# The last product of both down stages in two passes: two tiles first, then one tile after another

## The chip, the cores and the metric

One core of a Trainium2 chip runs the whole kernel. The metric is device time in microseconds (us) of one execution, median of several runs. Lower is better.

## The reference

A decoder layer on x of 2 x 512 tokens by 1024 features, in three parts: a state-space mixer with a gated feed-forward, a quantized product with a context matrix, and a second gated feed-forward whose weights are built from two arrays each. Both feed-forwards have 3584 inner features. In outline:

```python
x = x + mamba_and_gated_mlp(layernorm(x))   # silu(h2 @ gate_w.T) * (h2 @ up_w.T) @ down_w.T
x = x + quantized_product(layernorm(x), ctx_4096)   # fake_quant both, then matmul
# _L0_ffn_ref(layernorm(x), ...)
W1, W2, W3 = (base + mean(abs(w - base)) * sign(w - base) for each pair)
h = silu(hidden @ W1.T) * (hidden @ W3.T)   # 1024 tokens, 1024 -> 3584
x = x + h @ W2.T                            # 3584 -> 1024
```

All of it is fp32 within a small tolerance.

## The kernel before

Feature tiles of 128 lie on the partitions and tokens on the free axis. fp32 products are made of three rounded matmuls each (fp32r): high weight by high activation, high weight by low activation, low weight by high activation. ScalarE makes the high part of each operand by a copy, VectorE the low part by a subtraction.

The kernel runs in stages: head and mixer, feed-forward m=0, the context product, feed-forward m=1. A feed-forward has a gate-and-up part and a down part. The down stage uses a seven-product scheme on 2 x 2 blocks (Strassen's kind, with sums of blocks formed on VectorE), for two halves of the inner features (`sc` = 0 and 1), so it has 14 products, `d` = 0 to 13. One product has `SC_PAIRS` = 7 steps `k`, one for each pair of inner tiles, and `KH` = 4 output tiles `q` of 128 x 512, each in a bank of PSUM of its own: banks 0 to 3 for even `d`, 4 to 7 for odd `d`. In `down_step` (L1071) one step is 4 tiles of 3 matmuls, so a product is 7 x 12 = 84 matmuls.

Work orders:

- A step needs a slot of the weight ring (`ring_hi`, `ring_lo`; `RING` = 7) and one of the inner ring (`inner_ring_a`, `inner_ring_b`; 7 too). VectorE's `feed_forward` (L1949) and ScalarE's (L1458) fill the slots five or six steps ahead of TensorE, in an order written out by hand. A slot is refilled when its step of the product before is done (`s_pd`, one count per step; L1322, L1350, L1796).
- `down_out` (L1901) waits on VectorE for the end of a product and adds or subtracts its four tiles into x (`x_mid` for m=0, `x_last` for m=1), one instruction of 128 x 512 per tile (L1915), each with one count of `s_do`. TensorE needs these counts before it writes the banks again, two products later.
- At the end of m=1, SyncE stores each tile of the last quarter when its count of `s_do` is there (L736 to L740), and then the program ends.
- At the end of m=0, TensorE's order (L1155 to L1170) weaves the start of the context stage into the last product: the matmuls for a mean (L1157) stand before step 3, and the sums for a variance (`ctx_var`, L1119) before step 5. The mean waits for `s_xs`, which VectorE counts at the end of `x_sum_of` (L1965, L1994), done after `down_out` of product 12. The variance waits for four sums of squares, `square_pairs` (L2287) on VectorE, which come after `ctx_centre` (L2269), and that waits for the mean. After the last product TensorE does 64 small matmuls for column sums (L1111), the second mean (L1170, L1173, which wait for `s_do`), the first context products (L1125), column sums again and a second variance (L1119).
- VectorE leaves its feed-forward loop for m=0 six steps before the end (L1987), when the last slots are filled, and then goes through L2330 to L2337: centring, pairs, constants, root, two rounding steps (L2303), `down_out` of the last product, the other rounding steps. ScalarE's root for the second variance is L1619, behind a pass over the columns (L1635).
- SyncE loads `raw_even` (L685) for the next feed-forward when `s_pd` says that the whole down stage is done; VectorE uses it with the signs in L1947.

TensorE's order at the end of m=0:

```python
        feed_forward(BASE_G[0] + 2, W_END[0] - 4)
        pe.wait_ge(s_xs, 1)
        pe.matmul(bank(0), ones_mean[:, :], scr_c(4)[:, HALF[0]], start=True, stop=True).then_inc(s_hm, 1)
...
        feed_forward(W_END[0] - 4, W_END[0] - 2)
        ctx_var(bank(1), x_square_a, range(KH), KT, (), 0)
        feed_forward(W_END[0] - 2, W_END[0])
```

Of the kernel before, what the change touches and what calls it, by code (L numbers as in the profile page):

```python
# [11 lines left out]
P = 128  # L12
# [175 lines left out]
def build(nc, x_t, ctx, w_mamba, w_dt, w_gu, w_dn, f_gu, f_dn, b_gu, b_dn, params, shapes_only,  # L188
# [233 lines left out]
    s_dtm, s_dte, s_dts, s_csx = (sem(n) for n in ("dt_and_cs_summed", "dt_exp_in", "dt_and_cs_act", "cs_exp_in"))  # L422
    s_dtc = sem("dt_rows_copied")
    s_hpair = sem("head_pairs_summed")
# [33 lines left out]
    s_ld = [[sem(f"down_in{g}_{k}") for k in range(SC_PAIRS)] for g in range(2)]  # L458
    s_xq = [sem(f"x_quarter_in{i}") for i in range(4)]
    s_do, s_x2, s_out = sem("down_taken"), sem("x2_stored"), sem("out_stored")  # L460

# [364 lines left out]
    def _(pe):  # L826
# [72 lines left out]
        conv_pair(1)  # L899
        pe.wait_ge(s_dtc, 1)  # L900
        pe.wait_ge(s_ht, BATCH + 1)
# [113 lines left out]
        def product(w, m, p, t, x):  # L1015
# [53 lines left out]
            ins.then_inc(s_pd, 1)  # L1069

        def down_step(w, m, sc, t, k):  # L1071

            pe.wait_ge(s_wlo, w + 1)
            u = w - BASE_D[m]
            pe.wait_ge(s_ulo, m * ND + u + 1)
            d = sc * 7 + t
            if k == 0:
                if d >= 2:
                    pe.wait_ge(s_do, 4 * (m * 14 + d - 1))
                elif d == 0:  # L1080
                    pe.wait_ge(s_c12, 2 * (PAIRS - 1) * (m + 1))
                else:
                    pe.wait_ge(s_gs, 4 * PAIRS * (m + 1))
                    pe.wait_ge(s_pr[2], PAIRS * (m + 1))
                    if m == 0:
                        pe.wait_ge(s_ab, CF_BLOCKS)
            slot, us = w % RING, u % RING
            for q in range(KH):
                out = bank(4 * (d % 2) + q)
                col = slice(q * P, (q + 1) * P)  # L1090
                for n, (wt, a) in enumerate(((WRH, ur_hi(us)), (WRH, ur_lo(us)), (WRL, ur_hi(us)))):
                    ins = pe.matmul(out, wt[:, slot, col], a, start=t in (0, 1, 3) and k == 0 and n == 0,  # L1092
                                    stop=k == SC_PAIRS - 1 and n == 2, skip_group_check=True)
            ins.then_inc(s_pd, 1)
# [143 lines left out]
    def _(act):  # L1238
# [277 lines left out]
        act.wait_ge(s_dtm, 1)  # L1516
        act.activation(dt_rows, ps[2][0:2 * HEADS, :], ACT.Copy).then_inc(s_dtc, 1)
        root(1, scr_u)
# [164 lines left out]
    def _(dve):  # L1683
# [217 lines left out]
        def down_out(w):  # L1901
# [5 lines left out]
            for quad, op in {0: ((0, ALU.add),), 1: ((0, ALU.add),), 2: ((1, ALU.add),), 3: ((3, ALU.subtract),),  # L1907
                             4: ((3, ALU.subtract),), 5: ((1, ALU.add),), 6: ((2, ALU.subtract),)}[t]:
                dve.wait_ge(s_xq[quad], 16 * (m + 1))
                if d % 14:  # L1910
                    dve.wait_ge(s_do, 4 * d)
                dve.wait_ge(s_pd, w + 1)
                for q in range(KH):
                    tile = X[m][:, QROW[quad] + q, COL[m][QCOL[quad]]]
                    TT(tile, tile, bank(4 * ((sc * 7 + t) % 2) + q), op).then_inc(s_do, 1)  # L1915
# [206 lines left out]
        TS(ncs_all[:, :, :], ncs_all[:, :, :], -1.0, None, ALU.mult).then_inc(s_dte, 1)  # L2122
        dve.wait_ge(s_dts, 1)

# [7 lines left out]
        own.then(TT(ncs_all[:, :, :], ncs_all[:, :, :], dend_all[:, :, :], ALU.mult))  # L2132
        dve.wait_ge(s_dts, 3)
        own.then(TT(ncs_all[:, :, :], ncs_all[:, :, :], gtot_all[:, :, :], ALU.mult))
# [21 lines left out]
        conv_pair(CONV_TILES // 2 - 1, decay_rows)  # L2156
        dve.wait_ge(s_dts, 5)
        dve.wait_ge(s_silu, CONV_TILES)
# [279 lines left out]
```

## Time and profile before

| what | value |
|---|---|
| median of 3 runs | 2155.32 us (2153.18 to 2155.93) |
| the profiled execution | 2155.74 us, span of its instructions 2153.9 us |
| mean granted TensorE clock | 0.991 of 2.4 GHz |
| TensorE busy | 2105.2 us, 98% of the span |
| VectorE busy | 1664.3 us, 77% |
| ScalarE busy | 1070.0 us, 50% |
| DMA | 370.06 MB, mean 172 GB/s |

The times inside the profile are us from the start of the span. The first down stage ends at about 1260, the second at about 2149. A timeline row has its start, its length, the engine, the source line and operation, what was written and read, and how many instructions it merges; in brackets stands how long the engine sat idle before it, and who released it. The lengths of TensorE's matmuls overlap, so their pitch is read from the starts. "Granted clock" (PEclk) is the share of 2.4 GHz that TensorE was given: 1.00 is 2.4 GHz, 0.50 is 1.2 GHz.

### The profile page before, as it was taken

The page shows a single profiled execution, that of the slowest core. Times are in us where ns is not written, and L with a number is a line of the kernel's source. Part 1 is how long each engine was busy: PE and PEld are TensorE (multiplying, and loading weights), DVE is VectorE, ACT ScalarE, POOL GpSimd, SP SyncE. Part 2 cuts the span into 40 slices and gives each one's busy share as a digit, 9 for nine tenths or more (in the row PEclk, how much of TensorE's full clock was granted, in tenths as well). Part 3 has the DMA queues.
Part 4 walks back from the last instruction along what each step waited for, and adds up shares of the span by engine and source line. Part 5 has one row for each costly group of instructions (what it writes and reads, how often), then busy time and mean ns, then how long its engine had stood idle before and what let it go on. Part 6 is the DMA issues. An engine that isn't in the chain of part 4 may idle for free.

```text
span 2153.9 us, 26614 instructions
## 1 busy us (share of the span) xinstructions
PE 2105.2 (98%) x9266; PEld 1684.2 (78%) x9270; DVE 1664.3 (77%) x2497; ACT 1070.0 (50%) x1764; POOL 182.1 (8%) x296
## 2 busy tenths in 40 slices
PE   7999999999999999999999999899999999999999
PEld 3777778778888878888888854788888888888887
DVE  7776666698777878887979898887777677788885
ACT  4333344457777777774444466443333333444442
POOL 0000110101111111210000002001000000100000
PEclk9999999999999999999999999999999999999999
DMA  3151115638989999888250044554444444756101
GB/s 123 40 186 50 57 59 175 171 75 287 311 294 309 344 320 328 307 308 337 90 184 1 1 166 105 152 186 152 159 171 147 164 147 147 287 194 197 63 20 59
DMA packets 136434, 370.06 MB, mean 172 GB/s; under 512 B 16688, under 2 KB 27568, under 8 KB 132656
## 3 DMA queue, kind: packets, MB, share of 16 engines
q1 hardware_dynamic: 111216, 288.16, 39.1%
q0 software_dynamic: 25088, 80.23, 11.0%
q8 instruction: 73, 1.20, 0.2%
q14 instruction: 57, 0.47, 0.1%
HBM read 288.12 MB, written 84.41 MB: 173 GB/s over the span
## 4 chain that ended last, share of the span: by engine, by line
PE 82%; DVE 10%; ACT 4%; issue 2%; DMA 2%; SPq 0%; DVEq 0%; ACTq 0%
PE pair L1067 41%; PE pair L1092 24%; PE pair L839 6%; PE pair L832 2%; PE pair L1011 2%; DVE conv_out L2099 1%; DMA ctx_in<-ctx 1%; DVE ring_lo L1779 1%; PE pair L949 1%; DVE pair L1923 1%; PE pair L970 1%; PE pair L848 1%; DVE weights_lo L1689 1%; PE pair L1125 1%; PE pair L972 0%
## 5 line engine op out<-in xcount | busy, mean ns | idle before, releaser
L1067 PE MATMUL pair<-comb_hi,ring_hi 128*128 128x512 f32 x1456 | 567.3, 390 | 3.3 <-ACT gate_a L1401 3.3
L1067 PE MATMUL pair<-comb_hi,ring_lo 128*128 128x512 f32 x1456 | 567.2, 390 | 0.0
L1067 PE MATMUL pair<-comb_lo,ring_hi 128*128 128x512 f32 x1456 | 567.1, 389 | 0.0
L1092 PE MATMUL pair<-inner_ring_a,ring_hi 128*128 128x512 f32 x1120 | 344.8, 389 | 0.0
L1067 PEld LDWEIGHTS pair<-comb_hi,ring_hi 128*128 128x128 f32 x1456 | 273.7, 188 | 61.7 <-DVE ring_lo L1779 4.9
L1067 PEld LDWEIGHTS pair<-comb_hi,ring_lo 128*128 128x128 f32 x1456 | 273.7, 188 | 57.0
L1067 PEld LDWEIGHTS pair<-comb_lo,ring_hi 128*128 128x128 f32 x1456 | 273.7, 188 | 56.6
L1092 PEld LDWEIGHTS pair<-inner_ring_a,ring_hi 128*128 128x128 f32 x1120 | 210.2, 188 | 43.5
L1092 PE MATMUL pair<-inner_ring_a,ring_lo 128*128 128x512 f32 x560 | 217.9, 389 | 0.0
L1323 ACT ACTIVATE ring_hi<-ring_sum 128x512 fp32r<-128x512 f32 x160 | 101.0, 632 | 142.0 <-DVE ring_sum L1764 140.3
L1092 PE MATMUL pair<-inner_ring_b,ring_hi 128*128 128x512 f32 x448 | 138.3, 390 | 0.0
L1779 DVE TENSOR_TENSOR ring_lo<-raw_a,ring_hi 128x512 fp32r<-128x512 f32 x146 | 99.4, 685 | 50.1 <-ACT ring_hi L1323 50.1
L1449 ACT ACTIVATE sign_out<-pair 128x1024 int8<-128x1024 f32 x84 | 85.9, 1023 | 80.7 <-DVE pair L1923 80.7
L1092 PEld LDWEIGHTS pair<-inner_ring_a,ring_lo 128*128 128x128 f32 x560 | 105.1, 188 | 21.9
L839 PE MATMUL pair<-act_hi,weights_hi 128*128 128x512 f32 x256 | 109.3, 427 | 1.6 <-DVE act_lo L2168 1.4
L1779 DVE TENSOR_TENSOR ring_lo<-ring_sum,ring_hi 128x512 fp32r<-128x512 f32 x160 | 109.5, 684 | 1.5 <-ACT ring_hi L1323 0.2
L1923 DVE TENSOR_TENSOR pair<-coeff_in 128x1024 f32<-128x1024 f32 x84 | 103.0, 1226 | 0.8 <-DMA coeff_in<-b_gu 0.8
L1689 DVE TENSOR_TENSOR weights_lo<-weights_raw,weights_hi 128x1024 fp32r<-128x1024 f32 x44 | 54.6, 1240 | 59.5 <-ACT weights_hi L1246 31.1
L839 PE MATMUL pair<-act_hi,weights_lo 128*128 128x512 f32 x256 | 100.3, 392 | 0.0
L839 PE MATMUL pair<-act_lo,weights_hi 128*128 128x512 f32 x256 | 100.1, 391 | 0.0
L1092 PEld LDWEIGHTS pair<-inner_ring_b,ring_hi 128*128 128x128 f32 x448 | 84.1, 188 | 17.8 <-issue 0.5
L1323 ACT ACTIVATE ring_hi<-raw_a 128x512 fp32r<-128x512 f32 x146 | 90.3, 625 | 8.4 <-PE pair L1011 5.6
(374 smaller groups left out, 3586.1 us busy)
## 6 DMA issues: line engine op xcount, KB each, us to landing
coeff_in<-f_gu SPq DMA_DIRECT2D x56, 512.0 KB, 5.2
coeff_in<-b_gu SPq DMA_DIRECT2D x56, 512.0 KB, 6.8
weights_raw<-w_mamba SPq DMA_DIRECT2D x44, 512.0 KB, 3.4
raw_a<-w_gu SPq DMA_DIRECT2D x28, 512.0 KB, 7.3
raw_a<-w_gu SPq DMA_DIRECT2D x56, 256.0 KB, 6.3
u_spill<-gate_a POOLq DMA_DIRECT2D x56, 256.0 KB, 5.8
coeff_in<-f_dn SPq DMA_DIRECT2D x28, 512.0 KB, 4.4
coeff_in<-b_dn SPq DMA_DIRECT2D x28, 512.0 KB, 6.6
```

The costliest lines, as they stand in the source:

```text
L832: ins = pe.matmul(out[:, HALF[half]], w[:, wi, k * P:(k + 1) * P], a(half, k), start=k == 0 and n == 0, stop=k == KT - 1 and n == 2)
L839: ins = pe.matmul(out, w[:, wi, k * P:(k + 1) * P], a(b, k), start=k == 0 and n == 0, stop=k == KT - 1 and n == 2, skip_group_check=True)
L848: return pe.matmul(out[:, HALF[b]], ones[:, :], src[:, HALF[b]], start=first, stop=last)
L949: pe.matmul(ps[2][:, g * 512:(g + 1) * 512], bx_cur[:, 2 + g, :], xbc[:, 4 + g * HPG:4 + (g + 1) * HPG, b * SEQ + c * P:b * SEQ + (c + 1) ...
L1011: ins = pe.matmul(out, wt[:, slot, col], a, start=j % 2 == 0 and kk == 0 and n == 0, stop=j % 2 == 1 and kk == KH - 1 and n == 2, skip_gro ...
L1067: ins = pe.matmul(out, wt[:, slot, col], a, start=t in (0, 1, 3) and kk == 0 and n == 0, stop=kk == KH - 1 and n == 2, skip_group_check=True)
L1092: ins = pe.matmul(out, wt[:, slot, col], a, start=t in (0, 1, 3) and k == 0 and n == 0, stop=k == SC_PAIRS - 1 and n == 2, skip_group_chec ...
L1323: act.activation(WRH[:, slot, :], src, ACT.Copy).then_inc(s_whi, 1)
L1449: act.activation(sign_out[:, c % 2, :], dif_ps[:, :], ACT.Sign).then_inc(s_sign, 1)
L1689: TT(WL[:, slot, :], raw[:, rslot, :], WH[:, slot, :].bitcast(F32), ALU.subtract).then_inc(s_ready, 1)
L1779: TT(WRL[:, slot, :], src, WRH[:, slot, :].bitcast(F32), ALU.subtract).then_inc(s_wlo, 1)
L1923: TT(dif_ps[:, :], dif[:, c % 2, 0, :], dif[:, c % 2, 1, :], ALU.subtract).then_inc(s_cd, 1)
```

## The change

The last product of each down stage (`d` % 14 = 13) is done in two passes. While its seven slots come in, only tiles 0 and 1 are multiplied, 6 matmuls a step. Behind the last step tile 2 is done over all seven slots and then tile 3, 21 matmuls each. A new semaphore `s_last` counts when tiles 0 and 1 are done and when tile 2 is done; VectorE waits for it ahead of tiles 0 and 2, and for `s_pd` ahead of tile 3. The seven counts of `s_pd` for this product now come during tile 3. The orders of TensorE, VectorE and ScalarE around it are as they were. `s_dtc` is removed: its one count in the mixer goes to `s_dts`, whose later thresholds rise by one.

```diff
--- before.py
+++ after.py
@@ -420,7 +420,6 @@
     s_hs, s_hfree = sem("hs_ready"), sem("h_region_free")
     s_conv, s_silu = sem("conv_summed"), sem("conv_silu")
     s_dtm, s_dte, s_dts, s_csx = (sem(n) for n in ("dt_and_cs_summed", "dt_exp_in", "dt_and_cs_act", "cs_exp_in"))
-    s_dtc = sem("dt_rows_copied")
     s_hpair = sem("head_pairs_summed")
     s_stage, s_bx, s_rr = sem("chunk_stage_free"), sem("bx_chunk_ready"), sem("cs_rhs_ready")
     s_yt, s_cs, s_ecs, s_msk, s_dec = sem("y_taken"), sem("cs_rows"), sem("exp_cs"), sem("cs_masked"), sem("decay_ready")
@@ -457,6 +456,7 @@
     s_uo = [sem(f"inner_stored{i}") for i in range(4)]
     s_ld = [[sem(f"down_in{g}_{k}") for k in range(SC_PAIRS)] for g in range(2)]
     s_xq = [sem(f"x_quarter_in{i}") for i in range(4)]
+    s_last = sem("last_tiles_done")
     s_do, s_x2, s_out = sem("down_taken"), sem("x2_stored"), sem("out_stored")
 
     block = nc.Block()
@@ -897,7 +897,7 @@
                                 start=False, stop=k == KT - 1, skip_group_check=True)
         ins.then_inc(s_dtm, 1)
         conv_pair(1)
-        pe.wait_ge(s_dtc, 1)
+        pe.wait_ge(s_dts, 1)
         pe.wait_ge(s_ht, BATCH + 1)
         for t in range(NC):
             ins = pe.matmul(ps[3][:, t * 2 * HEADS:(t + 1) * 2 * HEADS], dt_rows[:, t * P:(t + 1) * P],
@@ -1068,6 +1068,21 @@
                                     stop=kk == KH - 1 and n == 2, skip_group_check=True)
             ins.then_inc(s_pd, 1)
 
+        def last_tiles(w, m, k, qs):
+            slot, us = w % RING, (w - BASE_D[m]) % RING
+            for q in qs:
+                out = bank(4 + q)
+                col = slice(q * P, (q + 1) * P)
+                for n, (wt, a) in enumerate(((WRH, ur_hi(us)), (WRH, ur_lo(us)), (WRL, ur_hi(us)))):
+                    ins = pe.matmul(out, wt[:, slot, col], a, start=False,
+                                    stop=k == SC_PAIRS - 1 and n == 2, skip_group_check=True)
+                if k == SC_PAIRS - 1 and q == 1:
+                    ins.then_inc(s_last, 1)
+                elif k == SC_PAIRS - 1 and q == 2:
+                    ins.then_inc(s_last, 1)
+            if qs == (3,):
+                ins.then_inc(s_pd, 1)
+
         def down_step(w, m, sc, t, k):
 
             pe.wait_ge(s_wlo, w + 1)
@@ -1084,6 +1099,14 @@
                     pe.wait_ge(s_pr[2], PAIRS * (m + 1))
                     if m == 0:
                         pe.wait_ge(s_ab, CF_BLOCKS)
+            if d % 14 == 13:
+
+                last_tiles(w, m, k, (0, 1))
+                if k == SC_PAIRS - 1:
+                    for q in (2, 3):
+                        for kk in range(SC_PAIRS):
+                            last_tiles(w - k + kk, m, kk, (q,))
+                return
             slot, us = w % RING, u % RING
             for q in range(KH):
                 out = bank(4 * (d % 2) + q)
@@ -1514,7 +1537,7 @@
 
         conv_silu(0, 0)
         act.wait_ge(s_dtm, 1)
-        act.activation(dt_rows, ps[2][0:2 * HEADS, :], ACT.Copy).then_inc(s_dtc, 1)
+        act.activation(dt_rows, ps[2][0:2 * HEADS, :], ACT.Copy).then_inc(s_dts, 1)
         root(1, scr_u)
         conv_silu(0, 1)
 
@@ -1909,8 +1932,15 @@
                 dve.wait_ge(s_xq[quad], 16 * (m + 1))
                 if d % 14:
                     dve.wait_ge(s_do, 4 * d)
-                dve.wait_ge(s_pd, w + 1)
+                if d % 14 < 13:
+                    dve.wait_ge(s_pd, w + 1)
                 for q in range(KH):
+                    if d % 14 == 13 and q == 0:
+                        dve.wait_ge(s_last, 2 * m + 1)
+                    elif d % 14 == 13 and q == 2:
+                        dve.wait_ge(s_last, 2 * m + 2)
+                    elif d % 14 == 13 and q == 3:
+                        dve.wait_ge(s_pd, w + 1)
                     tile = X[m][:, QROW[quad] + q, COL[m][QCOL[quad]]]
                     TT(tile, tile, bank(4 * ((sc * 7 + t) % 2) + q), op).then_inc(s_do, 1)
 
@@ -2120,7 +2150,7 @@
         own.then(TT(dtf, dtp[:, :, 1, :], dtf, ALU.add))
         own.then(STT(ncs_all[:, :, :], dtf, -1.0, dtf, ALU.mult, ALU.max))
         TS(ncs_all[:, :, :], ncs_all[:, :, :], -1.0, None, ALU.mult).then_inc(s_dte, 1)
-        dve.wait_ge(s_dts, 1)
+        dve.wait_ge(s_dts, 2)
 
         TS(a_all[:, :, :], ncs_all[:, :, :], 1.0, None, ALU.add).then_inc(s_dte, 1)
         dve.wait_ge(s_dte, 2)
@@ -2130,7 +2160,7 @@
         own.then(TS(dend_all[:, :, :], dend_all[:, :, :], 2.0 ** -30, None, ALU.max))
         own.then(dve.reciprocal(dend_all[:, :, :], dend_all[:, :, :]))
         own.then(TT(ncs_all[:, :, :], ncs_all[:, :, :], dend_all[:, :, :], ALU.mult))
-        dve.wait_ge(s_dts, 3)
+        dve.wait_ge(s_dts, 4)
         own.then(TT(ncs_all[:, :, :], ncs_all[:, :, :], gtot_all[:, :, :], ALU.mult))
         own.then(TT(ncs_all[:, :, :], ncs_all[:, :, :], sp1v, ALU.add))
         own.then(STT(dtf, dtf, 0.0, ncs_all[:, :, :], ALU.max, ALU.add))
@@ -2154,7 +2184,7 @@
             ins = dve.tensor_copy(cs_wide[:, :, first:first + HEADS], ncs_all[:, :, :])
         ins.then_inc(s_csx, 1)
         conv_pair(CONV_TILES // 2 - 1, decay_rows)
-        dve.wait_ge(s_dts, 5)
+        dve.wait_ge(s_dts, 6)
         dve.wait_ge(s_silu, CONV_TILES)
         def make_y(h, k):
             y = xbc[:, 4 + k, HALF[ORDER[h]]]
```

## Rows read from the trace of the kernel before

**Rows 1.** The page: busy time by engine, and the chain that ended last, by engine.

```profile
PE 2105.2 (98%) x9266; PEld 1684.2 (78%) x9270; DVE 1664.3 (77%) x2497; ACT 1070.0 (50%) x1764; POOL 182.1 (8%) x296
...
PE 82%; DVE 10%; ACT 4%; issue 2%; DMA 2%; SPq 0%; DVEq 0%; ACTq 0%
```

**Rows 2.** Timeline, TensorE, end of the first down stage: start us, length us, what.

```profile
1235.61 0.62 PE L1092 MATMUL pair<-inner_ring_a,ring_hi 128*128 128x512 f32 x2
...
1236.29 0.62 PE L1092 MATMUL pair<-inner_ring_a,ring_hi 128*128 128x512 f32 x2
...
1243.78 1.02 PE L1157 MATMUL pair<-scratch_c,ones_over_dm 128*128 128x512 f32 x2
...
1250.59 3.59 PE L1119 MATMUL pair<-x_mid,ones_over_dm 128*128 128x512 f32 x8
...
1259.51 1.75 PE L1111 MATMUL pair<-ones_bf,q 128*128 128x1 bf16 x64
...
1261.92 1.10 PE L1170 MATMUL pair<-scratch_c,ones_over_dm 128*128 128x512 f32 x2 [0.66 <-DVE x_mid L1915]
...
1276.49 1.75 PE L1111 MATMUL pair<-ones_bf,q 128*128 128x1 bf16 x64
...
1278.10 3.68 PE L1119 MATMUL pair<-x_mid,ones_over_dm 128*128 128x512 f32 x8
```

**Rows 3.** Timeline, VectorE, the same stretch.

```profile
1238.42 2.87 DVE L1994 TENSOR_TENSOR scratch_c<-scratch_c,x_mid 128x512 f32<-128x512 f32 x4
...
1243.62 0.68 DVE L1810 TENSOR_TENSOR inner_ring_b<-inner_ring_b_f,inner_ring_b 128x512 fp32r<-128x512 f32 x1
...
1244.84 4.87 DVE L2269 TENSOR_TENSOR centred<-x_mid,pair 128x512 f32<-128x512 f32 x8 [0.53 <-PE pair L1157]
...
1249.63 2.49 DVE L2287 TENSOR_TENSOR x_mid<-x_mid 128x512 f32<-128x512 f32 x4
...
1261.09 2.47 DVE L1915 TENSOR_TENSOR x_mid<-x_mid,pair 128x512 f32<-128x512 f32 x4
...
1280.23 2.46 DVE L1947 SCALAR_TENSOR_TENSOR raw_even<-sign_in_ab,coeff,raw_even 128x1024 f32<-128x1024 int8 x2
```

**Rows 4.** Timeline, VectorE, end of the program.

```profile
2134.52 0.68 DVE L1810 TENSOR_TENSOR inner_ring_b<-inner_ring_b_f,inner_ring_b 128x512 fp32r<-128x512 f32 x1
...
2148.75 2.48 DVE L1915 TENSOR_TENSOR x_last<-x_last,pair 128x512 f32<-128x512 f32 x4 [13.55 <-PE pair L1092]
```

**Rows 5.** What line 739 stored, and how long its transfers took.

```profile
L739 SPq DMA_DIRECT2D out_t<-x_last x16: 332/332/338, 2054.5 to 2151.3; - x16
...
DMA to landing us min/median/max: 2.0/2.2/2.3
```

**Rows 6.** Timeline, ScalarE, behind the second variance.

```profile
1279.55 2.56 ACT L1635 ACTIVATE centred<-centred,column_terms 128x512 f32<-128x512 f32 x4 [0.93 <-DVE column_terms L2310]
...
1282.02 0.66 ACT L1619 ACTIVATE scratch_c<-pair,quant_columns 128x512 f32<-128x512 f32 x1
```

**Rows 7.** Stretches: length, busy us by engine, PEclk, DMA share, GB/s.

```profile
13.10:15.20 2.10, 0.00 (x0) 0.00 (x0) 2.05 (x4) 0.63 (x2) 0.00 (x0) 1.00 1.06 403
...
15.30:19.00 3.70, 3.70 (x9) 1.76 (x10) 3.70 (x7) 3.70 (x7) 0.00 (x0) 1.00 0.82 322
...
25.80:29.90 4.10, 0.02 (x1) 0.00 (x0) 4.00 (x7) 1.20 (x3) 0.00 (x0) 0.81 0.22 68
...
29.90:35.10 5.20, 5.18 (x6) 2.18 (x7) 5.20 (x8) 4.17 (x7) 0.00 (x0) 0.50 0.12 49
...
1319.70:1321.50 1.80, 0.04 (x1) 0.00 (x0) 1.80 (x4) 1.26 (x2) 0.00 (x0) 1.00 0.29 107
...
1321.90:1325.40 3.50, 3.50 (x5) 1.35 (x4) 3.40 (x7) 1.41 (x3) 0.00 (x0) 0.51 0.14 53
...
1245.00:1259.50 14.50, 14.50 (x58) 10.43 (x57) 12.16 (x23) 6.71 (x11) 0.00 (x0) 1.00 0.84 291
```

**Rows 8.** Timeline, DMA queue, the load behind the first down stage.

```profile
1259.75 0.33 SPq L685 DMA_DIRECT2D raw_even<-b_gu  x1
```

## The prediction

> **What bounds the kernel now.** The page comes first: TensorE is busy 98% of the span and carries 82% of the chain that ended last [rows 1]. So time is won or lost where TensorE stands, or where the chain leaves it. The change touches two such places, and the timelines of TensorE and VectorE are read there: the end of the first down stage, which runs into the context stage, and the end of the second, which is the end of the program. In the first, three matmuls take 0.68 us (1235.61 to 1236.29), 0.227 each, and TensorE has a little work of the next stage woven in: the mean at 1243.78, the variance at 1250.59 [rows 2]. VectorE, not TensorE, holds the chain there: it comes to the four subtractions of the last product only at 1261.09, behind centring and rounding [rows 3], while TensorE had finished that product at 1259.51 [rows 2]. At the end of the program VectorE does wait for TensorE, 13.55 us, and then runs four subtractions from 2148.75 for 2.48 us, with a store after each [rows 4].
>
> **The second down stage: a gain.** The matmuls are the same 84 in another order, so TensorE ends at the same time unless a slot is late. Slots are now wanted every 6 matmuls (1.36 us) instead of every 12 (2.72). Counting back from 2148.7, the product begins 84 x 0.227 = 19.1 us earlier, at 2129.6. The last slot (number 6) is wanted at 2129.6 + 6 x 1.36 = 2137.8; VectorE starts its last piece at 2134.52 and needs 0.68, so it is ready at 2135.2 [rows 4], 2.6 us early; slot 5 was made 1.2 us before that and is wanted 1.36 us earlier, about as early. No stall: 0. After the last matmul one subtraction is left instead of four; they are 0.60 us apart (2.48 for four, the last 0.68), so 1.8 us go. The stores take 2.0 to 2.3 us to land [rows 5]; the last one now goes alone, which is worth 0 to 0.3 more. I take 1.8: the landings hardly differ. The first three stores go out earlier, under matmuls, on a queue that has nothing else then.
>
> **The first down stage: a loss.** The same order meets the woven-in work. TensorE starts the product at 1235.61. Three steps are now 18 matmuls, 4.1 us, so it stands at the mean at 1239.7. The mean needs the sum over x_mid, VectorE L1994, which ends at 1238.42 + 2.87 = 1241.29 [rows 3]. Idle 1: 1.6 us, where before TensorE came at 1243.78. The mean and its two small neighbours take 1243.78 to 1250.59 less 24 matmuls (5.44), 1.37 us; two steps of two tiles are 2.72 more: TensorE is at the variance at 1245.4.
>
> The variance needs the sums of pairs of squares, VectorE L2287. Centring (L2269) started at 1244.84 because it waited for the mean; its mean is now early, but VectorE must still finish the last slot (L1810, from 1243.62, next start 0.60 later), so centring moves only from 1244.84 to about 1244.3 [rows 3]. The first pair was done at 1249.63 + 0.68 = 1250.3 and now is at 1249.8. Idle 2: 1249.8 less 1245.4, 4.4 us. Before, TensorE covered this wait with whole steps; now each step has half as many matmuls in it, and tiles 2 and 3, which would have covered it, stand behind the variance. From here TensorE is continuous: variance 3.48 (1250.59 to 1259.51 less 5.44), two steps 2.72, tile 2 and tile 3 with 21 matmuls each, 4.76 apiece. End of the product: 1265.5 instead of 1259.5.
>
> Who waits: VectorE, at 0.5 us earlier than before, finds tiles 0 to 2 done and waits about 4 us for tile 3, with all its rounding (L2303) queued behind. TensorE itself goes on with 64 column sums (1.75 us) and comes to the second mean, which started at 1261.92 after 0.66 us of idling for VectorE [rows 2], at about 1267.3: 1.6 + 4.4 - 0.66 = 5.4 us later. Does that last? Up to 1278.10 TensorE has the means, the first products and the second column sums back to back (1261.92, 1276.49, 1278.10 [rows 2]), at its own pace, so the next variance is 5.4 us later too, and ScalarE's root (L1619) hangs on it. That root started at 1282.02, 0.2 us after the variance's last matmul (1278.10 + 3.68), but the column pass L1635 ahead of it ended only at 1282.11 [rows 6]: 0.3 us of slack. Everything up to the next feed-forward hangs on that root; I let 5.1 us through.
>
> **The clock.** A new idle stretch has a second price. The granted clock was full before the idle stretches of 4.1 us (at 25.8) and 1.8 us (at 1319.7); it then fell to 0.50 for 5.2 and 3.5 us of the work behind them, that is 1.2 GHz instead of 2.4; behind an idle stretch of 2.1 us (at 13.1) it stayed at 1.00 [rows 7]. Work at half clock loses half of that time: 1.7 to 2.6 us. For 4.4 us of idling I take 2.3, nearer the row of 4.1 us. The bounds are 0 (the row at 13.1) and 3.4 (two low stretches as at 1319.7). TensorE is continuous behind it, so it all arrives: the product ends near 1268. The Trainium skill (TensorE: Matmul & The Clock Gate, Part 1) says that the throttled state is the default and activity lifts it; its section on HAM oscillation warns of just such gaps inside a loop. By that rule alone the work behind Idle 2 would surely run at 1.2 GHz and rival (a) would have no chance; the trace agrees at 25.8 and 1319.7 and not at 13.1, so (a) keeps one. On the pitch of back-to-back matmuls the same page (Wait, 56ns, not 53.3ns?) gives 215.7 ns for 512 columns, where the rows show 227; an estimate by it puts the end of the product 0.6 us earlier, since 54 matmuls stand behind the variance, and the time at 2160.3.
>
> **The rest of the diff.** The product's counter s_pd now rises only during tile 3. Its waiters: no slot is refilled in this product (all seven are distinct, and the refills look at the product before); the next stage's weights come long after; SP's load of raw_even (1259.75 [rows 8]) waits for the whole product in both versions and moves by some 8 us with the sign and down loads behind it. They are 3.7 MB, 12.6 us at the 291 GB/s of the stretch before [rows 7], so down by about 1281, and L1947 uses them at 1280.23 [rows 3], itself some 7 us later: 0, with 0 to 1 as bounds. The two extra counter steps are carried by matmuls: 0. Merging s_dtc into s_dts changes only thresholds, in the same order: 0.
>
> **Sum.** -1.8 + 5.1 + 2.3 = +5.6 us. The profiled execution took 2155.74, so 2161.3; the median of the runs shown is 2155.32, 0.4 lower, so **2160.9 us**. A measurement of this kernel can tell about 0.2% (4.3 us) from no change; 5.6 is just beyond.
>
> **Rivals.**
> (a) The clock doesn't fall, or falls only inside the idle stretch: +3.3, 2158.6. For it: the row at 13.1, half as long. Against: the one stretch as long as this, at 25.8, was followed by a low clock, and so was the shorter one at 1319.7 [rows 7]. Chance 0.13.
> (b) The first stage's loss is hidden: if the chain from 1261 on were VectorE's and ScalarE's alone, with TensorE 5 to 8 us ahead of them, only the gain at the end would be left: -1.8, 2153.5. For it: VectorE holds the chain at 1261.09, and three of four tiles are ready for it. Against: TensorE is back to back from 1261.92 to 1278.10, and tile 3 itself is late for VectorE. It decides if TensorE has more than 8 us of slack before 1282; the rows show 0.3. This is the one that ends on the other side. Chance 0.15.
> (c) The late TensorE work costs more than once: a second low clock in the rounding stage, whose short matmuls leave gaps of their own, 1.7 us more, or late loads for L1947, 1 us: +7.3 to +8.3, up to 2163.6. Chance 0.1.
> (d) Slots 5 and 6 stall the second stage's last product: it decides if VectorE were 2.6 us later than it is, and then costs what is over. Chance 0.02; about 2162.
> The forecast keeps 0.6.
>
> **How the numbers follow.** The forecast's own spread is the clock term, 1.7 to 3.4 about 2.3, and about 1 us between executions: 2159.5 to 2163. With (a) and (d) that is 0.75; to hold 0.8 the range takes in most of (c) and the partly hidden cases towards (b): 2156.5 to 2163.5. Slower by over 4.3 us: nine tenths of the forecast (0.54), (c) and (d), 0.66. Faster by over 0.2% needs more than twice the end's gain with nothing lost, a quarter of (b): 0.04. The rest of (b), (a) and the forecast's tail are 0.30.
>
> **What will show it.** In the changed profile: TensorE idle about 1.6 us before L1157 and about 4.4 us before L1119, releaser VectorE; a granted clock of 0.5 behind the second; the last matmul of the product near 1268 and VectorE's fourth subtraction just behind it, apart from the third; L1619 about 7 us later; the gap kept until the next feed-forward; and at the end of the program a single subtraction after the last matmul. Wrong if TensorE's idling before L1119 is under 2 us, if the root at L1619 moves by less than 3, or if the second stage's last product has a gap.

## The result, and the profile after

The changed kernel takes **2158.94 us** (median of 13 runs, 2157.62 to 2162.62), the kernel before in the same series 2155.32 (13 runs, 2152.74 to 2158.77). The medians are 3.6 us apart; the ratio is 1.0021 with an interval of 1.0013 to 1.0028, which is 2.8 to 6.0 us slower about a middle of 4.5. The interval lies wholly above 1, so the kernel is slower, by about the 0.2% that the prediction called tellable. The forecast was 2160.9.

Two profiled executions can't be subtracted as they stand: everything ahead of the change came 1.40 us earlier in this one. The anchor used from here on is VectorE's four subtractions of the product before the last, 0.3 us behind the start of the last product. In the first down stage they start at 1235.91 before and 1234.51 after. Counted from this anchor A, the changed kernel differs like this:

| from A to | before | after | difference |
|---|---|---|---|
| end of the last product, first stage | 23.60 | 31.36 | +7.76 |
| ScalarE's root | 46.11 | 52.88 | +6.77 |
| the same subtractions of the second down stage | 893.80 | 900.60 | +6.80 |
| from those to VectorE's last subtraction or group of them | 19.04 | 18.94 | -0.10 |
| from the start of that to the end of the span | 5.15 | 3.15 | -2.00 |

With the 1.40 ahead of it: -1.40 + 6.80 - 0.10 - 2.00 = +3.30, the difference of the two spans (2157.2 and 2153.9). Without the 1.40, which the change did not bring, it is +4.7.

The page of the changed kernel, its busy times and its chain, answers to [rows 1]:

```profile
span 2157.2 us, 26618 instructions
...
PE 2108.3 (98%) x9270; PEld 1683.7 (78%) x9270; DVE 1664.7 (77%) x2497; ACT 1070.2 (50%) x1764; POOL 182.1 (8%) x296
...
PE 85%; DVE 9%; ACT 3%; issue 2%; DMA 1%; SPq 0%; DVEq 0%; ACTq 0%
```

Nothing of it tells where the time went; TensorE's share of the chain only rose from 82 to 85%. The timeline does. TensorE of the changed kernel at the end of the first down stage, in place of [rows 2] (line numbers have moved: L1077 is the two-pass product, L1180 the mean, L1142 the variance, L1134 the column sums, L1193 the second mean):

```profile
1234.21 0.62 PE L1077 MATMUL pair<-inner_ring_a,ring_hi 128*128 128x512 f32 x2
...
1239.95 1.12 PE L1180 MATMUL pair<-scratch_c,ones_over_dm 128*128 128x512 f32 x2 [1.50 <-DVE scratch_c L2024]
...
1248.34 5.40 PE L1142 MATMUL pair<-x_mid,ones_over_dm 128*128 128x512 f32 x8 [4.06 <-DVE x_mid L2317]
...
1265.87 1.75 PE L1134 MATMUL pair<-ones_bf,q 128*128 128x1 bf16 x64
...
1267.48 1.10 PE L1193 MATMUL pair<-scratch_c,ones_over_dm 128*128 128x512 f32 x2
...
1283.68 3.68 PE L1142 MATMUL pair<-x_mid,ones_over_dm 128*128 128x512 f32 x8
```

Two brackets are new: 1.50 us ahead of the mean and 4.06 us ahead of the variance, both released by VectorE. And the variance's eight matmuls take 5.40 us where they took 3.59. The bracket of 0.66 before the second mean is gone. VectorE in the same stretch, in place of [rows 3] (L1945 is a subtraction of the product from x, L2024 the sum over x_mid, L2299 centring, L2317 the squares):

```profile
1234.51 2.48 DVE L1945 TENSOR_TENSOR x_mid<-x_mid,pair 128x512 f32<-128x512 f32 x4 [0.85 <-PE pair L1115]
1237.03 2.87 DVE L2024 TENSOR_TENSOR scratch_c<-scratch_c,x_mid 128x512 f32<-128x512 f32 x4
...
1242.82 4.87 DVE L2299 TENSOR_TENSOR centred<-x_mid,pair 128x512 f32<-128x512 f32 x8
1247.60 2.50 DVE L2317 TENSOR_TENSOR x_mid<-x_mid 128x512 f32<-128x512 f32 x4
...
1259.23 1.28 DVE L1945 TENSOR_TENSOR x_mid<-x_mid,pair 128x512 f32<-128x512 f32 x2
...
1261.30 0.69 DVE L1945 TENSOR_TENSOR x_mid<-x_mid,pair 128x512 f32<-128x512 f32 x1 [0.80 <-PE pair L1077]
...
1266.06 0.69 DVE L1945 TENSOR_TENSOR x_mid<-x_mid,pair 128x512 f32<-128x512 f32 x1 [4.07 <-PE pair L1077]
...
1284.85 2.46 DVE L1977 SCALAR_TENSOR_TENSOR raw_even<-sign_in_ab,coeff,raw_even 128x1024 f32<-128x1024 int8 x2
```

VectorE is continuous from the anchor to the squares, so centring comes only 0.62 us sooner after the anchor (8.31 against 8.93) though its mean is there long before: VectorE sets the time of the variance, and TensorE, which now comes early, only waits longer. Tile 3 is the late one (4.07 us). The formation of the next weights (1284.85) waited for no load. The clock, in stretches of TensorE in the changed kernel (columns as in [rows 7]):

```profile
1244.30:1248.30 4.00, 0.00 (x0) 0.00 (x0) 4.00 (x8) 4.00 (x7) 0.00 (x0) 1.00 0.90 315
1248.30:1253.20 4.90, 4.86 (x9) 2.08 (x9) 4.49 (x10) 0.19 (x2) 0.00 (x0) 0.65 1.03 383
1253.20:1265.80 12.60, 12.60 (x56) 10.09 (x54) 5.80 (x9) 3.25 (x5) 0.00 (x0) 1.00 0.22 81
```

In the idle stretch itself the granted clock is still full; in the 4.9 us behind it, it is 0.65 on average, and then full again. Last the end of the program on VectorE of the changed kernel, in place of [rows 4]:

```profile
2135.11 2.48 DVE L1945 TENSOR_TENSOR x_last<-x_last,pair 128x512 f32<-128x512 f32 x4 [0.85 <-PE pair L1115]
...
2139.92 0.69 DVE L1833 TENSOR_TENSOR inner_ring_b<-inner_ring_b_f,inner_ring_b 128x512 fp32r<-128x512 f32 x1
...
2144.64 1.28 DVE L1945 TENSOR_TENSOR x_last<-x_last,pair 128x512 f32<-128x512 f32 x2 [4.03 <-PE pair L1077]
2149.30 0.69 DVE L1945 TENSOR_TENSOR x_last<-x_last,pair 128x512 f32<-128x512 f32 x1 [3.38 <-PE pair L1077]
2154.05 0.69 DVE L1945 TENSOR_TENSOR x_last<-x_last,pair 128x512 f32<-128x512 f32 x1 [4.07 <-PE pair L1077]
```

One subtraction is left behind the last matmul, and the span ends 3.15 us after its start, not 5.15 after that of a group of four. The product did not stall for slots: from A's counterpart in this stage (the four subtractions at 2135.11) to the last subtraction it is as long as before to 0.1 us.

### The profile page after: what moved, and what is told of

The parts are those of the page before. It is cut to its first block, busy times and chain, and to the rows that moved or that the text cites. A ratio compares the mean times of both kernels' runs of the same rounds, so it can differ in the third digit from the quotient of the medians.

```text
span 2157.2 us, 26618 instructions
## 1 busy us (share of the span) xinstructions
PE 2108.3 (98%) x9270; PEld 1683.7 (78%) x9270; DVE 1664.7 (77%) x2497; ACT 1070.2 (50%) x1764; POOL 182.1 (8%) x296
## 4 chain that ended last, share of the span: by engine, by line
PE 85%; DVE 9%; ACT 3%; issue 2%; DMA 1%; SPq 0%; DVEq 0%; ACTq 0%
PE pair L1067 42%; PE pair L1115 23%; PE pair L839 6%; PE pair L1011 2%; PE pair L832 2%; PE pair L1077 1%; DVE conv_out L2129 1%; PE pair L1148 1%; PE pair L1142 1%; PE pair L949 1%; PE pair L848 1%; DVE ring_lo L1802 1%; DVE pair L1953 1%; PE pair L970 1%; DVE weights_lo L1712 1%
## 5 line engine op out<-in xcount | busy, mean ns | idle before, releaser
L1115 PE MATMUL pair<-inner_ring_a,ring_hi 128*128 128x512 f32 x1040 | 320.0, 389 | 0.0
L1115 PEld LDWEIGHTS pair<-inner_ring_a,ring_hi 128*128 128x128 f32 x1040 | 195.2, 188 | 40.6
L1115 PE MATMUL pair<-inner_ring_a,ring_lo 128*128 128x512 f32 x520 | 202.3, 389 | 0.0
L1115 PE MATMUL pair<-inner_ring_b,ring_hi 128*128 128x512 f32 x416 | 128.0, 389 | 0.0
L1115 PEld LDWEIGHTS pair<-inner_ring_a,ring_lo 128*128 128x128 f32 x520 | 97.6, 188 | 20.3
L1346 ACT ACTIVATE ring_hi<-comb_hi_f 128x512 fp32r<-128x512 f32 x72 | 45.4, 630 | 94.4 <-PE pair L1115 48.4
```

The costliest lines, as they stand in the source:

```text
L1346: act.activation(WRH[:, slot, :], src, ACT.Copy).then_inc(s_whi, 1)
```

## The experiments

The theory: the second stage gains 1.8 to 2.0 us, the first loses about 5 by TensorE's idling for VectorE's statistics and about 2 by the low clock behind it, and both arrive at the end. The rival that ends on the other side: the loss of the first stage is hidden behind VectorE and ScalarE. Each median is of a kernel's own runs (number in brackets), its ratio against runs of the kernel before on the same chip (22 to 29 of them, one where there is no interval).

| kernel | median | ratio | interval | in us | root later by |
|---|---|---|---|---|---|
| m1_only | 2152.97 (11) | 0.9988 | 0.9979 to 0.9997 | -2.6 | +0.01 |
| m0_only | 2161.79 (6) | 1.0033 | 1.0021 to 1.0046 | +7.1 | +6.46 |
| count_only | 2154.53 (11) | 0.9998 | 0.9989 to 1.0007 | -0.4 | +1.50 |
| filled | 2157.62 (11) | 1.0012 | 1.0003 to 1.0021 | +2.6 | +5.08 |
| covered | 2153.63 (12) | 0.9996 | 0.9988 to 1.0005 | -0.9 | +0.75 |
| late | 2157.59 (10) | 1.0009 | 1.0000 to 1.0018 | +1.9 | +4.18 |
| mean_earlier | 2151.61 (11) | 0.9990 | 0.9982 to 0.9999 | -2.2 | -0.62 |
| one_first | 2152.27 (1) | | | | +0.01 |
| pair_last | 2153.70 (1) | | | | +1.52 |
| after_again | 2159.31 (11) | 1.0023 | 1.0014 to 1.0032 | +5.0 | +6.76 |
| mean_again | 2152.25 (12) | 0.9982 | 0.9973 to 0.9990 | -3.9 | -0.62 |

"In us" is the ratio's distance from 1 times 2155. "Root later by" is the distance from the anchor A to ScalarE's root in the profiled execution, less the 46.11 of before.

**The change in one stage alone.** `m1_only` keeps the two passes for the second down stage, `m0_only` for the first; the semaphore's thresholds follow.

```diff
-            if d % 14 == 13:
+            if d % 14 == 13 and m == 1:
...
```

> Only the second down stage's last product is done in two passes; the first is as before. Theory (the change is a gain of about 2 us at the end of the program and a loss of about 7 us at the end of the first down stage): 1.8 to 2.1 us faster than the kernel before, so a ratio near 0.999, and from the start of the last subtraction to the end of the span about 3.1 us instead of 5.2. Rival (splitting costs TensorE something of its own, so the loss is in both stages): no faster than the kernel before.

> Only the first down stage's last product is done in two passes. Theory: all of the loss and none of the gain, 5 to 7 us slower than the kernel before, with TensorE idle about 1.5 and 4.1 us in that product and full clock lost behind the second. Rival (the loss comes from elsewhere, or is mostly run to run): within 2 us of the kernel before.

TensorE and VectorE of m0_only, the variance of the first stage and the end of the program:

```profile
1249.87 5.11 PE L1142 MATMUL pair<-x_mid,ones_over_dm 128*128 128x512 f32 x8 [4.06 <-DVE x_mid L2317]
...
2155.22 2.48 DVE L1945 TENSOR_TENSOR x_last<-x_last,pair 128x512 f32<-128x512 f32 x4 [13.55 <-PE pair L1115]
```

The end of the program in m1_only, VectorE:

```profile
2145.61 0.69 DVE L1945 TENSOR_TENSOR x_last<-x_last,pair 128x512 f32<-128x512 f32 x1 [4.07 <-PE pair L1077]
```

The two halves come apart cleanly. m0_only has both new idle stretches and the low clock, and its program ends like that of the kernel before, with four subtractions; it is 4.5 to 9.9 us slower (middle 7.1, where 5 to 7 were expected). m1_only has the first stage of before (root 46.12 behind A) and 3.09 us from the last subtraction to the end; it is 0.6 to 4.5 us faster. Their sum, +4.5 by the ratios, is the change.

**The merged counter alone.** `count_only` is the kernel before with `s_dtc` merged into `s_dts` and nothing else.

```diff
-        act.activation(dt_rows, ps[2][0:2 * HEADS, :], ACT.Copy).then_inc(s_dtc, 1)
+        act.activation(dt_rows, ps[2][0:2 * HEADS, :], ACT.Copy).then_inc(s_dts, 1)
...
```

> Both down stages as before; only the count of the copied dt rows is merged into the other semaphore. Theory: no difference, within 1 us. Rival (the merge delays or advances the mixer): a difference of the medians above 1 us, seen in the profile ahead of 300 us.

No difference that can be measured: -0.4 us by the ratio, from -2.4 to +1.5. Its profiled execution has the root 1.5 us late all the same, and this is a lesson on single profiles. TensorE of count_only, the second mean, whose last eight matmuls run mostly at half speed (5.12 us, where the kernel before takes 3.60) without any change near them:

```profile
1260.18 5.12 PE L1172 MATMUL pair<-x_mid,ones_over_dm 128*128 128x512 f32 x8
```

**The clock, by filling the gap.** `filled` is the changed kernel with 17 matmuls more in the idle stretch ahead of the variance. They write the bank that the variance then starts afresh, so nobody reads them: they are added work, in the place where TensorE idles.

```diff
+        for _ in range(17):
+            pe.matmul(bank(1), WRH[:, (W_END[0] - 3) % RING, 0:P], ur_hi((ND - 3) % RING), start=True, stop=True, skip_group_check=True)
         ctx_var(bank(1), x_square_a, range(KH), KT, (), 0)
```

> The changed kernel with 17 matmuls (3.9 us) that nobody reads put into TensorE's idle stretch ahead of the variance in the first down stage; they write the bank that the variance then clears. They take no time from other work, only the idling. Theory (the clock is a term of its own): the granted clock stays at 1.00 through the variance, its eight records take 3.5 us instead of 5.3, and the kernel is about 1.8 us faster than the changed one. Rival (the clock falls all the same because of the work ahead, or the idle time alone is the price): same time as the changed kernel, within 0.5 us.

TensorE of filled, the added matmuls and the variance:

```profile
1244.28 4.01 PE L1186 MATMUL pair<-inner_ring_a,ring_hi 128*128 128x512 f32 x17
1248.50 3.70 PE L1142 MATMUL pair<-x_mid,ones_over_dm 128*128 128x512 f32 x8 [0.20 <-DVE x_mid L2319]
```

The variance starts at the same distance from the anchor (13.84 us, 13.83 in the changed kernel), and takes 3.70 instead of 5.40. The root comes 51.19 behind the anchor instead of 52.88. So 1.69 us of the loss are the clock, and 5.08 remain without it. By the ratios too filled lies between the two kernels (+2.6 against +4.5), but the intervals overlap, so it is the trace that shows this. In the profile filled is only 2.93 us late at the second down stage: it has 0.97 of the clock between 1300 and 1350, where before and the changed kernel have 0.93, so it also missed a low stretch there, far behind the edit; whether the edit brought that about is open. The Trainium skill (TensorE: Matmul & The Clock Gate, HAM oscillation — how this bites in real kernels) describes a matmul loop in which each wait for a DMA throttles TensorE, and advises an order of the loop that keeps TensorE warm. The trace agrees, for a wait for VectorE: behind the idle stretch the eight matmuls take 5.40 us, without it 3.70.

**The second idle stretch, by covering it.** `covered` takes useful work instead: before the variance it does the first five of the seven slots for tiles 2 and 3 too, and only the last two of them at the end.

```diff
+        for q in (2, 3):
+            for kk in range(5):
+                last_tiles(W_END[0] - 7 + kk, 0, kk, (q,))
         ctx_var(bank(1), x_square_a, range(KH), KT, (), 0)
...
-                        for kk in range(SC_PAIRS):
+                        for kk in range(5 * (m == 0), SC_PAIRS):
```

> The changed kernel, but in the first down stage tiles 2 and 3 are multiplied over slots 0 to 4 ahead of the variance, and over slots 5 and 6 behind it. Theory (the loss is that the tiles which would have covered TensorE's wait stand behind the variance): the idle stretch of 4.1 us ahead of the variance and its low clock are gone, the one of 1.5 us ahead of the mean stays; from the last subtraction of product 12 to ScalarE's root it is 46.5 to 47.2 us (before 46.1, changed 52.9), and the kernel is 1 to 1.5 us faster than the one before. Rival (two passes as such cost the first stage, whatever stands between them): the root is still 5 us late.

TensorE of covered:

```profile
1239.15 1.12 PE L1180 MATMUL pair<-scratch_c,ones_over_dm 128*128 128x512 f32 x2 [1.50 <-DVE scratch_c L2027]
...
1250.14 3.60 PE L1142 MATMUL pair<-x_mid,ones_over_dm 128*128 128x512 f32 x8
...
1259.04 1.75 PE L1134 MATMUL pair<-ones_bf,q 128*128 128x1 bf16 x64
```

No bracket ahead of the variance, 3.60 us for it, and the root is 6.02 us earlier than in the changed kernel. What stays is the first idle stretch: +0.75 at the root, once the 0.66 us that it used to idle before the second mean are paid back, and +1.31 at the second down stage. With the end's gain of 2.0 that makes -0.7 to -1.3. The ratio gives -0.9, from -2.6 to +1.1: covered is faster than the changed kernel, but not measurably faster than the kernel before, and that it is 1 to 1.5 faster, as expected, isn't shown. It is the order in the first product that costs, not the two passes as such.

**Does a late TensorE arrive? `late`** is the kernel before with 24 matmuls of 512 columns, which nobody reads, between the last product and the column sums. Its two waits are those that the column sums have in any case; it has no new wait for VectorE.

```diff
+        pe.wait_ge(s_m1, 1)
+        pe.wait_ge(s_q2[0], 16 * KT)
+        for _ in range(24):
+            pe.matmul(bank(0), q2[:, 0, 0:P], q2[:, 1, 0:H], start=True, stop=True, skip_group_check=True)
```

> The kernel before with 24 matmuls (5.44 us) that nobody reads behind the last product of the first down stage, ahead of the column sums; VectorE finds all its tiles in time, only TensorE is late. Theory (the context stage passes TensorE's lateness on, less about 1 us of slack): the root 4.3 to 4.8 us late, kernel about 4.5 us slower. Rival (b) of the prediction (the stage is VectorE's and ScalarE's chain with slack for TensorE, and the loss comes from the late fourth tile): under 1.5 us slower.

TensorE of late, the column sums and the second mean:

```profile
1263.97 1.74 PE L1111 MATMUL pair<-ones_bf,q 128*128 128x1 bf16 x64
...
1265.58 1.11 PE L1174 MATMUL pair<-scratch_c,ones_over_dm 128*128 128x512 f32 x2
```

The column sums come 28.77 behind the anchor, 5.17 later than before, the second mean 30.38, 4.37 later (0.66 of it was the old idle stretch), the root 50.29, **4.18 later**. That is what the rival denies: it would have had no more than a fraction of this at the root. It is a little under the 4.3 to 4.8 that were expected. At the second down stage 3.4 are left in the profile, and over the runs the ratio gives +1.9, from 0 to 3.9, where 4.5 were expected. The runs alone would thus leave room for the rival's "under 1.5 us"; what excludes it is the trace. Of the 0.7 that is given back in the profile, 0.55 is a shorter idle stretch of TensorE ahead of 1366.88 (5.88 us instead of 6.43); behind that matmul the distance stays (+3.45 there, +3.4 at the second down stage). Why the runs show still less than the profile was not found.

**A better place for the mean.** `mean_earlier` starts from m1_only. Its first product is that of the kernel before, with all four tiles a step, and the mean stands before step 2 instead of step 3.

```diff
-        feed_forward(BASE_G[0] + 2, W_END[0] - 4)
+        feed_forward(BASE_G[0] + 2, W_END[0] - 5)
...
-        feed_forward(W_END[0] - 4, W_END[0] - 2)
+        feed_forward(W_END[0] - 5, W_END[0] - 2)
...
```

> The second down stage as changed, the first as before, but TensorE does the mean ahead of step 2 instead of step 3. Theory (VectorE's centring waited 0.5 us for the mean, and the chain runs through it): centring starts 0.5 us earlier against the last subtraction of product 12, the root 0.3 to 0.5 us earlier, and the kernel is about 2.3 us faster than the one before, 0.4 faster than with only the second stage changed. Rival (TensorE now idles for the sum and is what is late): no gain over that kernel.

VectorE of mean_earlier, the anchor and centring, and under it ScalarE's root:

```profile
1234.54 2.48 DVE L1945 TENSOR_TENSOR x_mid<-x_mid,pair 128x512 f32<-128x512 f32 x4 [0.85 <-PE pair L1115]
...
1242.85 4.87 DVE L2299 TENSOR_TENSOR centred<-x_mid,pair 128x512 f32<-128x512 f32 x8
...
1280.03 0.69 ACT L1642 ACTIVATE scratch_c<-pair,quant_columns 128x512 f32<-128x512 f32 x1
```

Centring starts 8.31 behind the anchor, as in the changed kernel and 0.62 sooner than before, and all 0.62 arrive at the root. TensorE pays little for it: no idle stretch is shown ahead of the mean, and the column sums come 0.36 us later than before (23.96 behind the anchor, not 23.60). A part as small as 0.62 us can't be told by these runs: mean_earlier has -2.2 by its ratio and m1_only -2.6, so the step is shown by the trace and not by the medians. The kernel as a whole is faster than the kernel before (0.2 to 3.9 us) and than the changed one.

**Other ways to split the last product.** Both start from m1_only and had one run each. `one_first` takes one tile first and three behind it, `pair_last` does tiles 2 and 3 together over the slots.

```diff
-                last_tiles(w, m, k, (0, 1))
+                last_tiles(w, m, k, (0,))
...
-                    for q in (2, 3):
+                    for q in (1, 2, 3):
...
```

> Only the second down stage's last product is changed, and its first pass has one tile: 3 matmuls (0.68 us) a step, then tiles 1, 2 and 3 over all slots. Theory (slots 5 and 6 are ready 5 to 5.7 us after the product begins; in the change they are wanted later than that, here at 3.4 and 4.1): TensorE idles 1.3 to 1.8 us in two pieces in that product, and the end keeps the 2 us gain behind the last matmul, so 0.3 to 0.7 us of the gain is left. Rival (no stall since the slots are all made early): no idle, same as with two tiles first.

TensorE of one_first, the first tile of two late slots:

```profile
2130.88 0.70 PE L1077 MATMUL pair<-inner_ring_b,ring_hi 128*128 128x512 f32 x2 [1.17 <-DVE inner_ring_b L1833]
...
2132.08 0.70 PE L1077 MATMUL pair<-inner_ring_b,ring_hi 128*128 128x512 f32 x2 [0.27 <-DVE inner_ring_b L1833]
```

Slots wanted every 3 matmuls come too late: from the anchor's counterpart in the second stage to the last subtraction it takes 20.90 us instead of 18.94. That is 1.96 more, of which 1.44 stand in the two brackets, and by the trace it eats the whole gain of 2.0, where 0.3 to 0.7 us of it were expected to stay. Its one run (2152.27, with 2155.27 for the kernel before) can't tell this. Of the two splits, two tiles first is the one that VectorE's pace allows.

```diff
-                    for q in (2, 3):
-                        for kk in range(SC_PAIRS):
-                            last_tiles(w - k + kk, m, kk, (q,))
+                    for kk in range(SC_PAIRS):
+                        last_tiles(w - k + kk, m, kk, (2, 3))
...
-                    elif d % 14 == 13 and m == 1 and q == 2:
-                        dve.wait_ge(s_last, 2)
+                    elif d % 14 == 13 and m == 1 and q == 2:
+                        dve.wait_ge(s_pd, w + 1)
```

> Only the second down stage's last product is changed: tiles 0 and 1 first, then tiles 2 and 3 together, slot by slot, so two subtractions are left behind the last matmul. Theory (each subtraction that no longer stands behind it gives 0.6 us, the landing of the last store the rest): from the first subtraction behind the last matmul to the end of the span 3.6 to 3.8 us (before 5.2, one tile left 3.1). Rival (only the DMA queue matters): 3.1 or 5.2.

VectorE of pair_last, end of the program:

```profile
2148.07 1.28 DVE L1944 TENSOR_TENSOR x_last<-x_last,pair 128x512 f32<-128x512 f32 x2 [8.13 <-PE pair L1077]
```

Two subtractions are left behind the last matmul. From their start to the end it takes 3.83 us, between the 5.15 of four and the 3.15 of one, at 0.6 to 0.7 us for each subtraction. The gain at the end is this count and little else.

**Both again, on one chip.** `after_again` is the changed kernel, `mean_again` is mean_earlier.

> The changed kernel once more, to size the sum. Theory (the traces add up: 6.8 us lost by the end of the first down stage's wake, 2.05 us won at the end of the program): 4 to 5.5 us slower than the kernel before, and the second profile again has 52.4 to 53.1 us from the last subtraction of product 12 to the root. Rival (the first comparison's 3.6 us is the size, because the late stage gives some of it back): 3 to 4 us slower, with less than 6 us between the two products' ends against before.

> The kernel with the second stage changed and the mean one step earlier, once more. Theory: 2.0 to 2.9 us faster than the kernel before, centring about 8.3 us behind the last subtractions of product 12 begin (before 8.9). Rival (no gain that holds): within 1 us of the kernel before.

The changed kernel: root 52.87 behind A, and the second stage's subtractions at 900.34, against 52.88 and 900.60. Its ratio gives +5.0 (3.0 to 6.9), its median +3.5. Its trace shows one thing more. TensorE of after_again, the two idle stretches and a row between them:

```profile
1238.57 1.12 PE L1180 MATMUL pair<-scratch_c,ones_over_dm 128*128 128x512 f32 x2 [1.50 <-DVE scratch_c L2024]
...
1240.93 1.06 PE L1077 MATMUL pair<-inner_ring_a,ring_hi 128*128 128x512 f32 x2
...
1246.96 5.40 PE L1142 MATMUL pair<-x_mid,ones_over_dm 128*128 128x512 f32 x8 [2.48 <-DVE x_mid L2317]
```

And stretches of the same run (length, TensorE's busy us, PEclk, DMA share, GB/s):

```profile
1241.00:1242.00 1.00, 1.00 (x4) 0.50 0.00 0
...
1245.00:1246.00 1.00, 0.00 (x0) 1.00 1.04 256
...
1248.00:1249.00 1.00, 1.00 (x3) 0.50 1.01 367
```

In this execution the clock fell behind the first idle stretch too. TensorE lost 1.6 us there, idled 2.48 instead of 4.06 us ahead of the variance, and the variance still started 13.84 us behind the anchor and still took 5.40: here time that TensorE lost before a start that VectorE sets cost nothing.

mean_again is 3.5 us below the kernel before by the medians, 2.2 to 5.8 by the ratio, and **faster than both kernels**. That is more than the 2.0 to 2.9 that were expected, though they lie in the interval.

## Why the prediction was right

The case that was forecast is the one that came, and the time lies in its range, 2.0 us below the point. The time alone wouldn't show this: rival (a) had 2158.6, which is nearer to the measured 2158.94 than the forecast's 2160.9. The traces decide. Point by point:

- **The second stage.** Forecast 1.8; the end is 2.0 shorter. Three subtractions at 0.60 are 1.8 of it. The remaining 0.2 lies behind the last subtraction (2.46 us to the end of the span instead of 2.67); that it comes of the last store's going alone fits, but wasn't tested. No slot was late, as reckoned.
- **Idle 1.** Forecast 1.6, measured 1.50, released by the sum over x_mid.
- **Idle 2.** Forecast 4.4, measured 4.06. Its end was placed 13.9 us behind the anchor and came at 13.83; TensorE came to it 0.3 later than reckoned: the 30 matmuls and the mean up to there took 0.4 us more than their pitch gives, and Idle 1 was 0.1 shorter. For the end of the product this changes nothing, because VectorE sets the start of the variance; after_again, where TensorE came 1.6 us later still, bears it out.
- **The rest of the product.** 1.50 + 4.06 + 0.4 + 1.8 of clock = 7.76, the measured lateness of its end; forecast 8.3. Behind it 0.66 and about 0.3 were to be taken off; 0.99 was, leaving 6.77 at the root, against a forecast of 7.4.
- **The clock.** This is the term that was mis-sized: 2.3 forecast, with 1.7 and 2.6 as what the two rows would give; 1.8 by the variance's own length, 1.69 by filled. The low stretch cost what the one at 1319.7 does (3.5 us long), not what the one behind the 4.1 us at 25.8 does (5.2 us long), though the idle stretch was as long as the latter. In these rows the length of the idle stretch did not tell the length of what followed, nor, by after_again, whether it follows at all: of the five profiled executions with the 1.50 us stretch ahead of the mean, one had a low clock behind it.
- **It arrives.** 6.77 at the root, 6.80 at the second down stage. Rival (b) is out by the traces: late alone moves the root by 4.18 without any other change, though its runs, at 0 to 3.9 us, don't exclude a small effect on the time. That late later gave back more than the changed kernel did stays open.
- **Rival (a)** failed with the first low row, 0.65 of the clock over the 4.9 us behind the idle stretch. **(c)** did not come: L1977 waited for nothing, and 1300 to 1350 shows 0.93 of the clock in both. A second low clock exists in after_again, but ahead of the variance, where it cost nothing. **(d)** did not come either.
- **s_dtc and the counts:** for s_dtc nothing that can be measured, by count_only (-2.4 to +1.5 us). The two extra counter steps cost nothing that shows: the second stage's product, which has them too, is as long as before to 0.1 us.

The trace's sum is +6.80 - 0.10 - 2.00 = +4.7 where the forecast had +5.6: 0.5 from the clock, 0.2 from the end, the rest in small pieces. The medians say +3.6 and +3.5, the ratios +4.5 and +5.0; all lie in both intervals. That "slower by over 0.2%" came true was partly luck: 1.0021 is just over, and its interval goes to both sides of 1.002.

## What to carry to other kernels

Finishing output tiles one after another pays where nothing but taking them out of PSUM and storing them is left: it takes the subtractions of all but the last tile off the end, here 2.0 us. Where another stage's work is woven in at counted steps, the same reorder halves what each step covers: places that were chosen by the number of steps have to be set anew by the work between them, or the wait comes back, with the clock on top. So apply such a change per stage, and ask at each woven-in wait who sets its end; a mean handed in sooner helps only as far as the engine that uses it is free.

## What the runs showed of the hardware

TensorE's clock fell to half behind an idle stretch of 4.06 us, but not inside it (granted 1.00), and 17 unread matmuls in its place kept it full. It fell behind shorter ones too: in after_again behind 2.48 us (full again before it for only about a microsecond of work), and behind 1.50 us, where the changed kernel, m0_only, filled and covered, with the same 1.50 us, kept 1.00. So short idle stretches are a risk and no certainty. Single profiles also show low stretches that belong to no edit: count_only and pair_last had one near 1260 (5.12 and 5.29 us for eight matmuls that otherwise take 3.60), worth 1.5 us at the root, while the same work in the kernel before ran at full clock. A difference of 1.5 us between two profiles of this kernel thus proves nothing about an edit until the stretch that carries it is found in the trace.
